# A macaron block of MoE, Mamba and MoE on one core: Mamba's norm statistics in two groups, the first layer's gated sums in four PSUM banks among the first chunk's projections, half of the B diagonals on GpSimd

## Chip, cores, metric

One core of a Trainium2 chip. The metric is the device time of one execution in microseconds, lower is better; the time before is the median of three runs, 862.25 us (859.62 to 864.14).

## What is computed

The input X holds 4096 tokens (16 sequences of 256) of 128 features. Three layers follow, each on the layer norm of X and added to X:

```python
x = x + 0.5 * ffn(layernorm(x))        # mixture of experts
x = x + mamba(layernorm(x))
x = x + 0.5 * ffn(layernorm(x))

# ffn: 64 experts, top 3 of each token, capacity 64, hidden 512
logits = xf @ gate_w + gate_b
top_l, top_i = top_k(logits, 3); gates = softmax(top_l)
h = gelu(buf @ w1 + b1); y = h @ w2 + b2        # buf: tokens by expert
out[token] += gate * y[expert, place]

# mamba: 256 channels, 16 states, kernel 4
raw, gate = split(x @ W_in)
h = silu(causal_conv(raw) + conv_b)
ts, B, C = split(h @ W_x)
dt = softplus(ts @ W_dt + b_dt)
state[t] = exp(dt*A) * state[t-1] + dt*B*h       # per channel and state
y = (sum_n state*C + h*D) * silu(gate);  out = y @ W_out
```

## The kernel before

Five instruction streams are written out by hand, one for each engine and one for the DMA queue of SyncE, and meet at semaphores (`wait_ge`, `then_inc`; helper `wait`). Each engine takes its stream strictly in order, so the place of an operation in the program is its place in the queue.

**MoE layers** (`moe_sync`, `moe_scalar`, `moe_tensor`, `moe_vector`, `moe_pool`, argument f = 0 or 1). X lies in SBUF as 32 tiles of 128 tokens. After the experts' outputs were scattered to DRAM, SyncE loads them back in five pieces (`YK`, L364; pieces of 4, 4, 8, 8, 8 tiles, three rows k each). TensorE forms gated sums of three tiles out of four in PSUM, by matmuls with gate diagonals (L546, eight groups g, one PSUM bank for each), VectorE adds a group's sum to X (L688) and the fourth tile by three scalar products (L683); this is `moe_residual`. Together they are called "residual g" here, and L546's groups "sum g".

**The transition to Mamba.** In `mamba_vector`, `ln_vector` (L238) runs the residual of one group ahead of the norm statistics of the group before (`moe_residual_ahead`, L690): bn_stats (L243), bn_aggr (L246) for all 32 tiles, and then the inverse root with its 13 dependent steps on 32 columns (L258 to L267). After that VectorE fills pads (L1059 to L1061), and only then ScalarE's `mamba_scalar` passes its wait for `rstd` (L1023) and normalises the first chunk (L954). `mamba_tensor` waits for `pads` 4 (L889).

**Mamba** runs over eight chunks of 512 tokens, q = 0 to 7, as a software pipeline with 16 steps n a chunk, from q = -2. In iteration q the scans of chunk q run beside the preparation of chunks b = q+1 and f = q+2:

- f: ScalarE normalises four tiles (L954), TensorE transposes (L783), ScalarE copies (L962), TensorE projects the raw half in two parts (`raw`, L791), ScalarE copies with the bias (L970), VectorE adds the taps of the convolution (L1077, six), ScalarE applies silu (L981), TensorE projects x (`x_proj`, L804), ScalarE copies ts, B and C (L990, L993), TensorE projects dt (L822, two halves) and transposes B (`b_transposes`, L816), ScalarE makes the softplus (L1000 to L1004), VectorE finishes dt (L1083, two halves, steps 14 and 15).
- b: GpSimd multiplies dt by h (`dtu`, L1150), TensorE transposes that (L833), ScalarE copies (L1008), SyncE sends dt and C through DRAM to spread them over partitions (L771, L775, L751, L760).
- q: in each step TensorE forms dt·B·h of a step by 64 small matmuls against the B diagonals (`dbu`, L849) two steps ahead, ScalarE the decays (L1019) four steps ahead, VectorE scans (L1097), GpSimd multiplies the states by C (`times_c`, L1143), TensorE sums over the states (`sum_states`, L871) once four such products are there.

The **B diagonals** are four tensors of 128x1024 a chunk, `dB[b % 2][:, k]`: a constant pattern `fold64` times B's transposed columns, each spread over 64. VectorE makes all four, straight from PSUM bank 4: k = 0 and 1 in steps 14 and 15 of iteration f-2, each ahead of the dt of that step, k = 2 and 3 in steps 0 and 1 of the next:

```python
if n <= 1 and back:
    diagonal(b, 2 + n)
...
if n >= 14 and front:
    diagonal(f, n - 14)
    dt(f, n - 14)
```

A scan waits for the product of GpSimd two scans back (three state buffers), `dbu` for the scan two steps back (two pairs of PSUM banks).

## Time and profile before

| | |
|---|---|
| median of three runs | 862.25 us (859.62 to 864.14) |
| the profiled execution | 867.32 us |
| its span, first to last instruction | 865.6 us |
| busy in the span | TensorE 683.7, VectorE 623.0, GpSimd 462.6, ScalarE 419.1 us |
| mean granted TensorE clock | 0.886 of 2.4 GHz |
| first MoE layer with its sums | 0 to about 209 us |
| Mamba, first normalisation to last product | 218.62 to about 651.6 us |
| second MoE layer | about 652 to 865.6 us |

The rows below give start, duration, engine, line of the kernel, operation and tiles. Durations of neighbours on one engine overlap a little, so costs are taken from start to start where they can. PE is TensorE's matmul, PEld its weight load, DVE VectorE, ACT ScalarE, POOL GpSimd. An idle time in brackets names what released the engine.

### The profile page before, as it was taken

Reading aid. Unit: us, or ns where it says so; the run is one execution under the profiler, and the core shown is the slowest. Engines: PE = TensorE matmul, PEld = TensorE weight load, DVE = VectorE, ACT = ScalarE, POOL = GpSimd, SP = SyncE. Lnnn points to the kernel's source line nnn. Section 1 sums busy time; section 2 is a strip of 40 time slices with the busy share of each in tenths; the row PEclk is TensorE's granted clock in tenths of the full one; section 3 lists DMA queues with packets and bytes.
Section 4 is the critical chain, followed back from the end, with each engine's and each line's share of the span. In section 5 each row is a group of like instructions: output and inputs, shape, how many; then the busy total and the mean of one; then the engine's idle time right before and its main releaser. Section 6 shows DMA issues by size and latency. Waiting matters only on the chain. (4 is left out here: it accounts for less than half of the span.)

```text
span 865.6 us, 27705 instructions
## 1 busy us (share of the span) xinstructions
PE 683.7 (79%) x11818; PEld 426.1 (49%) x11818; DVE 623.0 (72%) x1053; ACT 419.1 (48%) x779; POOL 462.6 (53%) x301
## 2 busy tenths in 40 slices
PE   5637999956456889899798989978886537999967
PEld 3625555545123445446454644545453525555546
DVE  7782555529246989899998989898996891555525
ACT  2410544420457867758676766756531320444520
POOL 3003666420013878798787778878992003566520
PEclk9857999979558999999999999989996757999979
DMA  8992999443055363443425353442004901999537
GB/s 289 396 322 74 341 378 300 160 153 153 5 167 182 120 201 103 140 153 111 154 92 183 111 155 137 114 153 97 3 4 158 396 29 47 329 379 308 181 112 295
DMA packets 92100, 155.47 MB, mean 180 GB/s; under 512 B 7315, under 2 KB 32541, under 8 KB 90704
## 3 DMA queue, kind: packets, MB, share of 16 engines
q1 hardware_dynamic: 87568, 141.40, 48.0%
q0 software_dynamic: 4416, 12.39, 4.1%
q8 instruction: 90, 1.47, 0.7%
q14 instruction: 26, 0.21, 0.1%
HBM read 112.02 MB, written 41.99 MB: 178 GB/s over the span
## 5 line engine op out<-in xcount | busy, mean ns | idle before, releaser
L1143 POOL TENSOR_TENSOR BIG<-BIG,R 128x1024 f32<-128x1024 f32 x128 | 301.1, 2372 | 65.5 <-DVE BIG L1097 65.4
L1097 DVE TENSOR_TENSOR_SCAN BIG<-BIG,ps 128x1024 f32<-128x1024 f32 x128 | 286.0, 2271 | 4.2 <-PE ps L849 2.9
L849 PE MATMUL ps<-BIG,stack 64*32 64x128 f32 x8192 | 154.1, 282 | 48.6 <-DVE BIG L1097 46.8
L849 PEld LDWEIGHTS ps<-BIG,stack 64*32 64x32 f32 x8192 | 118.9, 108 | 125.4 <-DVE BIG L1097 100.7
L1019 ACT ACTIVATE BIG<-BIG,An 128x510 f32<-128x510 f32 x192 | 124.0, 708 | 10.2 <-DVE BIG L1097 9.7
L717 POOL DMA_INDIRECT R<-xn_dram,tok_idx x64 | 65.2, 1019 | 100.7 <-DVE row_idx L645 80.9
L731 POOL DMA_INDIRECT y_dram<-BIG,row_idx x64 | 64.6, 1010 | 69.0 <-DVE BIG L669 63.3
L654 DVE COPY BIG<-ps 128x512 f32<-128x512 f32 x64 | 44.3, 692 | 74.1 <-PE ps L501 74.1
L390 ACT ACTIVATE BIG<-BIG 128x512 f32<-128x512 f32 x64 | 40.4, 631 | 104.9 <-DVE BIG L661 104.9
L871 PE MATMUL ps<-BIG,fold 128*32 128x512 f32 x512 | 70.1, 623 | 5.0 <-POOL BIG L1143 5.0
L501 PE MATMUL ps<-BIG 128*64 128x512 f32 x240 | 68.6, 651 | 0.0
L527 PE MATMUL ps<-BIG 128*64 128x128 f32 x960 | 65.7, 279 | 0.0
L1150 POOL TENSOR_TENSOR state_more<-state_more,BIG 128x512 f32<-128x512 f32 x16 | 20.4, 1274 | 82.3 <-DVE state_more L1083 82.3
L1065 DVE TENSOR_TENSOR BIG<-fold,ps 128x1024 f32<-128x1024 f32 x32 | 38.4, 1204 | 35.1 <-PE ps L816 35.1
L511 PEld LDWEIGHTS ps<-ident,BIG 128*128 128x128 f32 x256 | 36.0, 209 | 52.5 <-issue 52.5
L527 PEld LDWEIGHTS ps<-BIG 128*64 128x64 f32 x960 | 51.2, 136 | 4.0
L384 ACT ACTIVATE BIG<-ps 128x128 f32<-128x128 f32 x64 | 16.8, 262 | 68.8 <-PE ps L491 68.3
L511 PE MATMUL ps<-ident,BIG 128*128 128x128 f32 x256 | 48.5, 313 | 0.0
L661 DVE TENSOR_TENSOR BIG<-ps,b1T 128x512 f32<-128x512 f32 x64 | 44.3, 692 | 4.1 <-PE ps L511 1.4
L1077 DVE SCALAR_TENSOR_TENSOR BIG<-ps,vcol,BIG 128x506 f32<-128x506 f32 (+2 forms) x48 | 34.8, 739 | 14.3 <-ACT BIG L970 13.6
L479 PE MATMUL ps<-BIG 128*64 128x64 bf16 x384 | 24.7, 308 | 24.9 <-DVE BIG L607 24.9
L1019 ACT ACTIVATE BIG<-R,An 128x510 f32<-128x510 f32 x64 | 41.5, 710 | 1.8 <-DVE BIG L1097 1.7
(153 smaller groups left out, 972.4 us busy)
## 6 DMA issues: line engine op xcount, KB each, us to landing
BIG<-in_L_ffn_w SPq DMA_DIRECT2D x120, 512.0 KB, 6.3
dt_dram<-state_more SPq DMA_DIRECT2D x16, 1024.0 KB, 4.3
BIG<-dt_dram SPq DMA_DIRECT2D x48, 256.0 KB
BIG<-y_dram SPq DMA_DIRECT2D x18, 512.0 KB, 9.2
R<-c_dram SPq DMA_DIRECT2D x32, 256.0 KB
y_dram<-zeros SPq DMA_DIRECT2D x3, 2048.0 KB, 17.3
y_dram<-zeros SPq DMA_DIRECT2D x6, 1024.0 KB, 9.7
xn_dram<-R POOLq DMA_DIRECT2D x2, 2048.0 KB, 11.0
```

The source lines that it names most:

```text
L501: last = nc.tensor.matmul(ps[a * CAP:(a + 1) * CAP, 1 + s % 2, :], xt[s % 2][:, a * CAP:(a + 1) * CAP], w1s[b][:, a, :], start=True, stop= ...
L511: last = nc.tensor.transpose(ps[:, 3 + s % 2, c * P:(c + 1) * P], hs[s % 2].rearrange("n (p c) -> n c p", c=HC)[:, c, :], ident[:, :])
L527: last = nc.tensor.matmul(ps[a * CAP:(a + 1) * CAP, 5 + s % 2, 0:D], hT[s % 2][:, c, a * CAP:(a + 1) * CAP], w2s[b][:, a, c, :], start=Fal ...
L654: nc.vector.tensor_copy(hs[s % 2], ps[:, 1 + s % 2, :]).then_inc(S("hs"), 1)
L661: nc.vector.tensor_tensor(hb[s % 2].rearrange("p (c n) -> p c n", n=CAP), ps[:, 3 + s % 2, :].rearrange("p (c n) -> p c n", n=CAP), bias, ...
L717: nc.gpsimd.indirect_dma_start(xg[s], None, xn_dram[f], bass.IndirectOffsetOnAxis(tok_idx[:, j:j + 1].bitcast(U32), 0), bounds_check=T - 1 ...
L731: nc.gpsimd.indirect_dma_start(y_dram[f], bass.IndirectOffsetOnAxis(row_idx[:, j:j + 1].bitcast(U32), 0), yo[s], None, bounds_check=K * T ...
L849: last = nc.tensor.matmul(ps[CW * slot:CW * slot + CW, 2 * (st % 2) + b, :] .rearrange("p (g s k) -> p k g s", g=2, k=4)[:, k], dT[q % 2][ ...
L871: last = nc.tensor.matmul(ps[CW * j:CW * j + CW, 4 + h, :], fold32[:, :], prod[(st + j) % RP][:, :, g, :], start=False, stop=(gp == 1 and ...
L1019: last = nc.scalar.activation(dA[:, st % 6, :, g, 1:SEQ], dtR[cg][:, :, 1:SEQ], ACT.Exp, scale=An4[:, cg, 2 * gp + g:2 * gp + g + 1])
L1097: nc.vector.tensor_tensor_scan(state[st % 3], dA[:, st % 6].rearrange("p b g t -> p (b g t)"), ps[:, u:u + 2, :].rearrange("p b n -> p (b ...
L1143: nc.gpsimd.tensor_tensor(prod[st % RP], state[st % 3].rearrange("p (b g t) -> p b g t", b=2, g=2), Cf[q % 2][:, 2 * gp:2 * gp + 2].rearra ...
```

## The change

- **Statistics in two groups.** The root moves into `inverse_root(e, S, i0, i1, n)`, for any range of tiles. VectorE's Mamba stream takes residuals 0 and 1, the statistics and root of tiles 0 to 7, residuals 2 to 4; in iteration q = -2 it takes residual 5 at step 7, residuals 6 and 7, the last pad and the statistics of tiles 8 to 31 at step 9 (behind the taps), and their root at step 15, ahead of the second dt. Three pads come first. ScalarE waits for the first root ahead of chunk 0 and for the second ahead of chunk 2.
- **Sums in four banks.** In the first layer TensorE's sums leave `moe_tensor`: groups 0 to 3 run ahead of the Mamba iteration, group 4 at step 3 (behind the first transposes), 5, 6 and 7 at steps 6 to 8 (behind the raw projections). Group g uses bank g % 4 in both layers and waits, from group 4, for residual g-4.
- **B diagonals.** ScalarE copies B's transposed columns from PSUM to the new SBUF tile `BT` (128x64) at step 14, between the two softplus parts. VectorE makes k = 0 and 1 from `BT` at steps 0 and 1, GpSimd k = 2 and 3 at steps 3 and 9, each ahead of its product. Steps 14 and 15 of VectorE have none.

The diff, without the lines that only move the root's steps:

```diff
@@ -133,6 +133,7 @@
         fold32 = sb("fold32", [P, CW])
+        BT = sb("BT", [P, 4, NS])
@@ -152,11 +153,11 @@
         row_idx = sb("row_idx", [P, PAIRS], I32)
+        rs = sb("rs", [P, 3, NI])
         rows = small[0:E, 0:H]
-        rs = small[:, 512:608].rearrange("p (m i) -> p m i", m=3)
@@ -226,14 +227,34 @@
         moe_sems, ln_sems = Sems(ctx, nc, "e"), Sems(ctx, nc, "l")
+        MST = M.again(0, STAT_TOTALS)
         LNS = [ln_sems.again(n, LN_TOTALS) for n in range(2)]
-        LST = [ln_sems.again(n, STAT_TOTALS) for n in range(3)]
+        LST = [ln_sems.again(n, STAT_TOTALS) for n in range(2)]
+        def inverse_root(e, S, i0, i1, n):
+            def step(instruction):
+                nonlocal n
+                n += 1
+                instruction.then_inc(S("rstd"), 1)
+                e.wait_ge(*S.at("rstd", n))
+            v, y, z, r = rs[:, 0, i0:i1], rs[:, 1, i0:i1], rs[:, 2, i0:i1], rstd[:, i0:i1]
+            step(nc.vector.tensor_scalar(v, mv[:, i0:i1, 1], EPS, None, ALU.add))
...
+            step(nc.vector.scalar_tensor_tensor(out=nmr[:, i0:i1], in0=mv[:, i0:i1, 0], scalar=-1.0, in1=r,
+                                                op0=ALU.mult, op1=ALU.mult))
@@ -245,27 +266,9 @@
...
             e.wait_ge(*S.at("meanvar", NI))
...
+            inverse_root(e, S, 0, NI, 0)
@@ -364,7 +367,7 @@
         def moe_scalar(e, S, LS, f, between=None):
-            ln_scalar(e, LS, LST[2 * f])
+            ln_scalar(e, LS, LST[f])
@@ -537,19 +540,26 @@
-            e.wait_ge(*S.at("gdiag", MOE_TOTALS["gdiag"]))
-            e.wait_ge(*S.at("yo", PAIRS))
-            for g in range(8):
-                e.wait_ge(G(f"yk{PIECE[g]}"), 16 * K * (f + 1))
-                for i in range(4 * g, 4 * g + 3):
-                    for k in range(K):
-                        last = nc.tensor.matmul(ps[:, g, (i % 4) * P:(i % 4 + 1) * P],
-                                                gdiag[k][:, P * i:P * i + P], YK[:, k, i, :],
-                                                start=(k == 0), stop=(k == K - 1))
-                last.then_inc(S("sum"), 1)
+            if f == 1:
+                for g in range(8):
+                    gate_sums(e, S, f, g)
+        def gate_sums(e, S, f, g):
+            if g == 0:
+                e.wait_ge(*S.at("gdiag", MOE_TOTALS["gdiag"]))
+                e.wait_ge(*S.at("yo", PAIRS))
+            e.wait_ge(G(f"yk{PIECE[g]}"), 16 * K * (f + 1))
+            if g >= 4:
+                e.wait_ge(*S.at("x", g - 3))
+            for i in range(4 * g, 4 * g + 3):
+                for k in range(K):
+                    last = nc.tensor.matmul(ps[:, g % 4, (i % 4) * P:(i % 4 + 1) * P],
+                                            gdiag[k][:, P * i:P * i + P], YK[:, k, i, :],
+                                            start=(k == 0), stop=(k == K - 1))
+            last.then_inc(S("sum"), 1)
         def moe_vector(e, S, LS, f, before_stats=None):
-            ln_vector(e, LST[2 * f], before_stats)
+            ln_vector(e, LST[f], before_stats)
@@ -685,17 +695,7 @@
                     t = X[:, 4 * g:4 * g + 3, :].rearrange("p i d -> p (i d)")
-                    nc.vector.tensor_tensor(t, t, ps[:, g, 0:3 * D], ALU.add).then_inc(S("x"), 1)
-        def moe_residual_ahead(e, S, i):
-            if i % 4 == 0:
-                if i == 0:
-                    moe_residual(e, S, 0, 0)
-                if i + 4 < NI:
-                    moe_residual(e, S, 0, i // 4 + 1)
-                e.wait_ge(*S.at("x", i // 4 + 1))
-                e.wait_ge(*S.at("x4", K * (i // 4 + 1)))
+                    nc.vector.tensor_tensor(t, t, ps[:, g % 4, 0:3 * D], ALU.add).then_inc(S("x"), 1)
@@ -756,6 +756,8 @@
                     wait(e, "prod", STEPS * (b - 1))
+                    if b == 0:
+                        e.wait_ge(*F[0].at("sum", 8))
@@ -811,7 +813,7 @@
                 wait(e, "y", 2 * b - 3)
-                wait(e, "diag", 4 * b)
+                wait(e, "BT", b)
@@ -839,8 +841,11 @@
                 wait(e, "scanned", st - 1)
+                if st == 0:
+                    e.wait_ge(*F[0].at("x", 8))
                 if n == 0:
-                    wait(e, "diag", 4 * q + 4)
+                    wait(e, "diag", 2 * q + 2)
+                    wait(e, "diag_pool", 2 * q + 2)
@@ -855,7 +860,7 @@
                 if h == 0:
-                    wait(e, "diag", min(4 * NQ, 4 * q + 8))
+                    wait(e, "BT", min(NQ, q + 2))
@@ -886,7 +891,9 @@
-            e.wait_ge(M("pads"), 4)
+            for g in range(4):
+                gate_sums(e, F[0], 0, g)
+            e.wait_ge(M("pads"), 3)
@@ -904,6 +911,8 @@
                         transposes(f)
+                    if q == -2 and n in (3, 6, 7, 8):
+                        gate_sums(e, F[0], 0, max(4, n - 1))
@@ -949,6 +958,8 @@
                 wait(e, "t_psum", q)
+                if q in (0, 2):
+                    wait(e, "rstd", STAT_TOTALS["rstd"] * (1 + q // 2))
@@ -1003,6 +1014,13 @@
+            def bt_copy(b):
+                wait(e, "bt_psum", b + 1)
+                wait(e, "diag", 2 * b)
+                wait(e, "diag_pool", 2 * b)
+                nc.scalar.activation(BT[:, :, :], ps[:, 4, 0:4 * NS].rearrange("p (k n) -> p k n", k=4), ACT.Copy)\
+                    .then_inc(M("BT"), 1)
@@ -1015,13 +1033,16 @@
                 wait(e, "scanned", st - 5)
+                if st == 0:
+                    e.wait_ge(*F[0].at("sum", 8))
+                    e.wait_ge(*F[0].at("x4", K * 8))
+                    wait(e, "pads", 4)
-            e.wait_ge(*LST[1].at("rstd", STAT_TOTALS["rstd"]))
-            e.wait_ge(M("pads"), 4)
+            e.wait_ge(M("pads"), 3)
@@ -1048,22 +1069,55 @@
                     if n == 14 and front:
+                        bt_copy(f)
         def mamba_vector(e):
-            ln_vector(e, LST[1], lambda i: moe_residual_ahead(e, F[0], i))
+            def stats(i0, i1):
+                for i in range(i0, i1):
+                    if i % 4 == 0:
+                        e.wait_ge(*F[0].at("x", i // 4 + 1))
+                        e.wait_ge(*F[0].at("x4", K * (i // 4 + 1)))
+                    nc.vector.bn_stats(st[:, i, :], X[:, i, :]).then_inc(M("stats"), 1)
+                for i in range(i0, i1):
+                    wait(e, "stats", i + 1)
+                    nc.vector.bn_aggr(mv[:, i, :], st[:, i, :]).then_inc(M("meanvar"), 1)
+            def statistics(i0, i1, n):
+                wait(e, "meanvar", i1)
+                inverse_root(e, MST, i0, i1, n)
             nc.vector.memset(ts[DTR:DTR + 1, :], 1.0).then_inc(M("pads"), 1)
-            nc.vector.memset(dA[:, :, :, :, 0:1].rearrange("p u b g t -> p (u b g) t"), 0.0).then_inc(M("pads"), 1)
+            for g in range(2):
+                moe_residual(e, F[0], 0, g)
+            stats(0, 8)
+            statistics(0, 8, 0)
+            for g in range(2, 5):
+                moe_residual(e, F[0], 0, g)
+            def rest_of_moe(n):
+                if n == 7:
+                    moe_residual(e, F[0], 0, 5)
+                if n == 9:
+                    for g in range(6, 8):
+                        moe_residual(e, F[0], 0, g)
+                    e.wait_ge(*F[0].at("sum", 8))
+                    e.wait_ge(*F[0].at("x4", K * 8))
+                    nc.vector.memset(dA[:, :, :, :, 0:1].rearrange("p u b g t -> p (u b g) t"), 0.0).then_inc(M("pads"), 1)
+                    stats(8, NI)
+                if n == 15:
+                    statistics(8, NI, STAT_TOTALS["rstd"])
             def diagonal(b, k):
-                wait(e, "bt_psum", b + 1)
+                wait(e, "BT", b + 1)
+                wait(e, "dbu", STEPS * (b - 1))
                 nc.vector.tensor_tensor(dB[b % 2][:, k], fold64[:, :].unsqueeze(1).broadcast_to([P, NS, 64]),
-                                        ps[:, 4, NS * k:NS * k + NS].unsqueeze(2).broadcast_to([P, NS, 64]), ALU.mult)\
+                                        BT[:, k, :].unsqueeze(2).broadcast_to([P, NS, 64]), ALU.mult)\
@@ -1098,15 +1152,18 @@
-            wait(e, "pads", 4)
                 for n in range(STEPS):
+                    if q == -1 and n == 0:
+                        wait(e, "pads", 4)
+                    if q == -2:
+                        rest_of_moe(n)
                     if n <= 1 and back:
-                        diagonal(b, 2 + n)
+                        diagonal(b, n)
@@ -1117,7 +1174,6 @@
                     if n >= 14 and front:
-                        diagonal(f, n - 14)
@@ -1150,10 +1206,21 @@
+            def diagonal(b, k):
+                wait(e, "BT", b + 1)
+                wait(e, "dbu", STEPS * (b - 1))
+                nc.gpsimd.tensor_tensor(dB[b % 2][:, k], fold64[:, :].unsqueeze(1).broadcast_to([P, NS, 64]),
+                                        BT[:, k, :].unsqueeze(2).broadcast_to([P, NS, 64]), ALU.mult)\
+                    .then_inc(M("diag_pool"), 1)
                         dtu(q + 1, n)
+                    if n in (3, 9) and q + 1 >= 0 and q + 1 < NQ:
+                        if q == -1:
+                            e.wait_ge(*F[0].at("sum", 8))
+                        diagonal(q + 1, 2 + n // 9)
```

## Rows read from the trace of the kernel before

**Rows 1.** Stretches (busy us and instruction count of each engine; at the end PEclk, DMA share, GB/s).

```profile
184.00:218.62 34.62, 18.13 (x144) 17.78 (x144) 22.50 (x113) 0.00 (x0) 0.00 (x0) 0.80 0.49 183
...
218.62:244.30 25.68, 12.96 (x20) 4.58 (x20) 7.94 (x11) 14.21 (x23) 1.26 (x1) 0.50 0.12 23
...
244.30:271.00 26.70, 16.86 (x158) 9.18 (x158) 10.29 (x12) 18.12 (x29) 2.54 (x2) 0.68 0.52 168
...
271.00:319.40 48.40, 37.14 (x1107) 20.87 (x1108) 45.49 (x31) 36.05 (x57) 37.93 (x17) 0.96 0.52 175
...
369.00:418.60 49.60, 43.60 (x1157) 25.12 (x1142) 46.69 (x33) 35.55 (x56) 40.11 (x19) 0.98 0.42 135
...
567.40:609.20 41.80, 36.79 (x1072) 21.72 (x1056) 39.24 (x23) 26.32 (x39) 37.87 (x18) 0.95 0.29 104
...
609.20:651.60 42.40, 34.35 (x1048) 20.41 (x1048) 37.17 (x20) 20.15 (x29) 40.30 (x18) 0.95 0.01 3
```

**Rows 2.** Timeline of the transition (start us, us, engine line op out<-in xcount [idle before <-releaser]).

```profile
196.69 0.49 PE L546 MATMUL ps<-BIG,R 128*128 128x128 f32 x2 [1.04 <-DMA BIG<-y_dram]
...
196.81 0.87 DVE L243 BATCH_NORM_STATS2 st<-X 128x6 f32<-128x128 f32 x4
...
208.41 0.61 PE L546 MATMUL ps<-BIG 128*128 128x128 f32 x4
...
209.78 0.87 DVE L243 BATCH_NORM_STATS2 st<-X 128x6 f32<-128x128 f32 x4
...
212.19 0.86 DVE L243 BATCH_NORM_STATS2 st<-X 128x6 f32<-128x128 f32 x4
...
213.25 0.84 DVE L243 BATCH_NORM_STATS2 st<-X 128x6 f32<-128x128 f32 x4
...
214.66 0.18 DVE L258 TENSOR_SCALAR stack<-mv 128x32 f32<-128x32 f32 x1
...
217.61 0.08 DVE L1059 MEMSET R<- 128x6 f32 x2
...
218.62 1.65 ACT L954 ACTIVATE R<-X,nmr,rstd 128x128 f32<-128x128 f32 x4 [37.86 <-DVE BIG L1061]
```

**Rows 3.** The same timeline, the chain of chunk 0.

```profile
220.41 1.09 PE L783 MATMUL ps<-ident,R 128*128 128x128 f32 x4 [11.39 <-ACT R L954]
...
222.66 3.78 PE L791 MATMUL ps<-R,Wr 128*128 128x512 f32 x4 [1.16 <-ACT R L962]
...
225.66 4.53 DVE L1077 SCALAR_TENSOR_TENSOR BIG<-ps,vcol,BIG 128x506 f32<-128x506 f32 x6 [7.16 <-ACT BIG L970]
...
231.33 3.73 PE L804 MATMUL ps<-BIG,Wx 128*96 128x512 f32 x4 [4.89 <-ACT BIG L981]
...
243.61 0.69 DVE L1083 SCALAR_TENSOR_TENSOR state_more<-ps,state_more 128x512 f32<-128x512 f32 x1
```

**Rows 4.** VectorE's timeline, the end of chunk 1's chain and the first scan.

```profile
270.40 0.69 DVE L1083 SCALAR_TENSOR_TENSOR state_more<-ps,state_more 128x512 f32<-128x512 f32 x1 [1.21 <-ACT state_more L1004]
...
271.00 2.28 DVE L1097 TENSOR_TENSOR_SCAN BIG<-BIG,ps 128x1024 f32<-128x1024 f32 x1
```

**Rows 5.** Timeline of a full chunk: TensorE, ScalarE, VectorE.

```profile
384.43 1.07 PE L871 MATMUL ps<-BIG,fold 128*32 128x512 f32 x8
...
387.41 1.53 DVE L1077 SCALAR_TENSOR_TENSOR BIG<-ps,vcol,BIG 128x506 f32<-128x506 f32 x2 [0.21 <-ACT BIG L970]
...
410.71 0.63 ACT L1004 ACTIVATE state_more<-state_more 128x512 f32<-128x512 f32 x1
...
412.25 0.65 PE L816 MATMUL ps<-ident,R 16*128 16x16 f32 x4
...
412.94 1.22 DVE L1065 TENSOR_TENSOR BIG<-fold,ps 128x1024 f32<-128x1024 f32 x1 [2.63 <-PE ps L816]
```

**Rows 6.** Groups of instructions by line (busy us, mean ns of one, idle before, releaser).

```profile
L1143 POOL TENSOR_TENSOR BIG<-BIG,R 128x1024 f32<-128x1024 f32 x128 | 301.1, 2372 | 65.5 <-DVE BIG L1097 65.4
...
L1065 DVE TENSOR_TENSOR BIG<-fold,ps 128x1024 f32<-128x1024 f32 x32 | 38.4, 1204 | 35.1 <-PE ps L816 35.1
```

More of the change, by code:

```diff
@@ L235, in macaron @@
         w2v = w2.rearrange("(a j) (p c) d -> j p a (c d)", a=2, c=HC)
+        def inverse_root(e, S, i0, i1, n):
[6 more added lines that the diff above has]
+            step(nc.vector.tensor_scalar(v, mv[:, i0:i1, 1], EPS, None, ALU.add))
+            step(nc.vector.tensor_single_scalar(z.bitcast(I32), v.bitcast(I32), 1, ALU.arith_shift_right))
+            step(nc.vector.tensor_scalar(r.bitcast(I32), z.bitcast(I32), -1.0, float(0x5F3759DF), ALU.mult, ALU.add))
+            for k in range(3):
+                step(nc.vector.tensor_tensor(y, r, r, ALU.mult))
+                step(nc.vector.scalar_tensor_tensor(out=z, in0=y, scalar=-0.5, in1=v, op0=ALU.mult, op1=ALU.mult))
+                step(nc.vector.scalar_tensor_tensor(out=r, in0=z, scalar=1.5, in1=r, op0=ALU.add, op1=ALU.mult))
+            step(nc.vector.scalar_tensor_tensor(out=nmr[:, i0:i1], in0=mv[:, i0:i1, 0], scalar=-1.0, in1=r,
+                                                op0=ALU.mult, op1=ALU.mult))
         def ln_vector(e, S, before_stats=None):
@@ L246, in ln_vector @@
                     nc.vector.bn_aggr(mv[:, i, :], st[:, i, :]).then_inc(S("meanvar"), 1)
-            n = 0
-            def step(instruction):
-                nonlocal n
-                n += 1
-                instruction.then_inc(S("rstd"), 1)
-                e.wait_ge(*S.at("rstd", n))
-            v, y, z = rs[:, 0, :], rs[:, 1, :], rs[:, 2, :]
-            e.wait_ge(*S.at("meanvar", NI))
-            step(nc.vector.tensor_scalar(v, mv[:, :, 1], EPS, None, ALU.add))
-            step(nc.vector.tensor_single_scalar(z.bitcast(I32), v.bitcast(I32), 1, ALU.arith_shift_right))
-            step(nc.vector.tensor_scalar(rstd[:, :].bitcast(I32), z.bitcast(I32), -1.0, float(0x5F3759DF),
-                                         ALU.mult, ALU.add))
-            for k in range(3):
-                step(nc.vector.tensor_tensor(y, rstd[:, :], rstd[:, :], ALU.mult))
-                step(nc.vector.scalar_tensor_tensor(out=z, in0=y, scalar=-0.5, in1=v, op0=ALU.mult, op1=ALU.mult))
-                step(nc.vector.scalar_tensor_tensor(out=rstd[:, :], in0=z, scalar=1.5, in1=rstd[:, :],
-                                                    op0=ALU.add, op1=ALU.mult))
-            step(nc.vector.scalar_tensor_tensor(out=nmr[:, :], in0=mv[:, :, 0], scalar=-1.0, in1=rstd[:, :],
-                                                op0=ALU.mult, op1=ALU.mult))
+            e.wait_ge(*S.at("meanvar", NI))
+            inverse_root(e, S, 0, NI, 0)
         def ln_normalise(e, S):
```

## Prediction

> **What bounds the kernel now.** I read the stretches first [rows 1]. From the first state scan to the last product the Mamba part takes 380.6 us (271.00 to 651.60). In a full chunk VectorE is busy 46.69 of 49.60 us, TensorE 43.60, GpSimd 40.11, ScalarE 35.55. VectorE sets the pace, with the other two close behind. The last two stretches, where no projections are left, have GpSimd at 37.87 of 41.80 and 40.30 of 42.40: there it is GpSimd. Ahead of the scans lie 26.70 and 25.68 us in which no engine is busy for more than 19 us: a chain from engine to engine, at a granted clock of 0.68 and 0.50 (1.2 GHz in all of the second stretch). Before those, 34.62 us with ScalarE and GpSimd idle, in which VectorE adds the expert outputs and makes the statistics of all 32 tiles.
>
> The timeline of that transition [rows 2] shows the order to be broken: ScalarE's first normalisation starts at 218.62, although the tiles that it needs were complete on VectorE at 196.81. TensorE's last gated sum ends at 209.0. The timeline of a full chunk [rows 5] shows the one stall of VectorE in it: 2.63 us ahead of the first diagonal of step 14, released by the B transposes on TensorE.
>
> **The change, part by part. 1: the early start.** VectorE now takes residuals 0 and 1 (done at 196.81 in both kernels), eight tiles of statistics, then the root. Four tiles of statistics and aggregates take 213.25-212.19 = 1.06, so 2.1 to 198.9. The root takes 217.61-214.66 = 2.95 for 32 columns; eight columns shorten it little, I take 2.8, so 201.7. ScalarE starts at 201.8, 16.8 us earlier than at 218.62. Its four activations take 1.65: 203.5.
>
> TensorE meanwhile: six groups of sums took 209.0-196.69 = 12.3, 2.05 each, at full clock. Groups 2 and 3 end at 200.8, then it waits 2.7 us. Transposes at 203.5 take 0.7 (half of [rows 3] rounded up; 1.09 there at 1.2 GHz), sum 4 2.0 to 206.2, both raw projections half of 3.78 = 1.9 to 208.1, sum 5 to 210.2, sums 6 and 7 to 214.3.
>
> VectorE: a residual costs 212.19-209.78-1.06 = 1.35. Residuals 2 and 3 end at 204.5; residual 4 waits for sum 4 and ends at 207.4. From the end of the first raw half to the first tap there are 1.1 us (222.66+1.9 to 225.66 [rows 3]), the copy on ScalarE: 208.2. Taps, 4.53 for six: two to 209.7; residual 5 waits for sum 5, ends 211.4; four taps to 214.4. Before, x_proj followed the taps by 1.14 (230.19 to 231.33), took 3.73 at 1.2 GHz, and the second dt started 8.55 after its end (243.61), with a diagonal in between. Now: 215.6, 217.5 at full clock (219.3 at 1.2 GHz), and a second dt that is ready by 226.0 (227.9).
>
> Behind those taps VectorE carries the work that it did ahead of them before: residuals 6 and 7 (2.7), a memset (0.1), 24 tiles of statistics (6.4): 223.6. Then dt of the first half (0.7), the second root (2.95), dt of the second half (0.7): it starts at 227.2 and ends at 227.9. So the cover that the early start gave is used up by VectorE itself; ScalarE and TensorE, even with x_proj at 1.2 GHz, are just in time. Before, this dt ended at 243.61+0.69 = 244.30. **Part 1 gives 16.4 us.** If TensorE runs the transposes, sums 4 and 5 and the raw projections at 1.2 GHz, they take 0.4+4.1+1.9 = 6.4 us more, and the gain is 10.
>
> The chain of chunk 1 up to the first scan (26.70 [rows 4]) stays. On it ScalarE gets the BT copy, at most the 0.4 us that one of the four activations at 218.62 takes: 0.25.
>
> **2: four PSUM banks.** Sums 4 to 7 now wait for residuals 0 to 3. In the first layer these are done by 204.5; in the last layer the sums follow their loads (the last group of sums is released by the last load, residual 3 is long done). Nothing. The scratch tile `rs` costs nothing; the new waits on SyncE and ScalarE (for `sum` 8, `x4`, `pads`) are met by 224, over 20 us ahead of their users.
>
> **3: the diagonals, chunks 0 to 5.** Steps 14 and 15 of VectorE lose a diagonal each. At step 14 the dt can start once ScalarE has its softplus, 410.71+0.63 = 411.34, instead of after the stall and the diagonal (412.94+1.14 = 414.08). It ends at 411.95. Step 15's scan ends at 414.15. The second softplus now waits for the B transposes (412.25+0.65) and the copy of BT, and comes to 415.0; its dt ends at 415.6. The next chunk's scan started at 418.60. So 2.95 us less, 46.65 a chunk, if GpSimd keeps up.
>
> GpSimd gets two products of 128x1024 a chunk. Nearest row: 2.37 [rows 6] for the same size in f32 from SBUF. Its inputs here are both broadcast; bounds 1.2 (VectorE's own time for it) and 4.7 (twice). I take 2.37, the row of the same engine and size. Busy then 40.11+4.74 = 44.85 of 46.65: tight. Its first diagonal stands ahead of product 3. Product 2 starts when scan 2 ends, 8.8 us into the chunk (three scans of 2.2 and two diagonals of 1.1; the starts overlap the durations by under 0.1), so product 3 ends at 8.9+3x2.35 = 15.95. TensorE wants it for the sum that started 15.4 into the chunk (384.43-369.00), behind which the raw projection and the tap at 387.41 are queued. The tap moves by 0.55, and the chunk becomes 47.2.
>
> **4: two engines at one memory.** VectorE's diagonals read BT from SBUF now, no longer from PSUM. In a chunk every VectorE instruction of before takes one input at most from SBUF as a tensor, while GpSimd is busy 81% of the time; no row shows a VectorE instruction with two SBUF tensors beside a GpSimd product. Bounds for each of the two meetings a chunk: 0 (no effect), and 2.37, a whole product. I take 1.1, the diagonal's own length, borne by GpSimd: VectorE's diagonal follows its scan at once, and the product that waits for that scan's semaphore comes second. Then product 0 starts at 3.35 instead of 2.3 and the next diagonal pushes by 1.1 again: product 3 ends at 17.4, 2.0 behind the 15.4, and a chunk takes 48.65.
>
> The Trainium skill, page "SBUF — State Buffer", section "Who interferes with whom", speaks against this change: a VectorE instruction with two SBUF inputs and a GpSimd instruction that reads SBUF shut each other out for the whole instruction, whoever comes first. By it the sum would be as above, or 2 to 3 us dearer where GpSimd comes first. No run here shows it yet.
>
> **5: the sum.** First scan: 227.9+26.7+0.25+1.1 (GpSimd's second dtu meets a VectorE diagonal) = 256.0, **15.0 earlier**. Chunk 0 has no Mamba residual (0.6) and took 48.40: now 48.1, 0.3 less. Chunks 1 to 5: 5x(49.60-48.65) = 4.7. In chunk 6 VectorE saves nothing and GpSimd has 37.87+4.74+1.1 = 43.7 for 41.80: 1.9 worse; chunk 7 starts with GpSimd about 1 us further behind: 1.0 worse. Together 15.0+5.0-2.9 = 17.1. The profiled execution took 867.32 (span 865.6), 5.1 above the median 862.25; its 850.2 is 845 on the scale of the median.
>
> **The rivals.** *A, no meeting cost.* A chunk takes 47.2 (chunk 0 46.6): 16.1+1.8+5x2.4-2.1 = 27.8, **835**. For it: VectorE's diagonal, 1.20 on the mean [rows 6] with GpSimd mostly busy, takes 1.22 at 412.94, where GpSimd has nothing to do. Against it: that diagonal reads PSUM.
>
> *B, the clock.* TensorE idles 2.7 us at 200.8 and its clock, full until the end of the sums before (0.80 mean in the first stretch, 0.50 in the next), could fall by then. 6.4 less: **851**.
>
> *C, slower than before.* GpSimd's product of two broadcast inputs costs more than 2.37. Each extra us sits twice in seven chunks, behind product 3 and product 9; of the two about 1.5 come through in a chunk: 10 us in all. At 4.1 us a diagonal the 17 us are gone, at the bound of 4.7 it is 845+23 = **868**. For it: no row has such inputs. Against it: Cf's product has four-dimensional inputs already, and takes 2.37.
>
> *D, the change doesn't do what it says.* The statistics of the other 24 tiles stand ahead of dt in VectorE's order, so the early start only moves the wait. With both roots and a late softplus on top of one another part 1 gives 9 or less, and with meetings of 2.4 us nothing comes from the chunks: within 4 us of before, **859**.
>
> **How the numbers follow.** Forecast (840 to 850) 0.50, A 0.23, B 0.12, D 0.08, C 0.07. A measurement of this kernel can tell about 0.5%, 4.3 us. Faster by more than that (below 857.9): the forecast, A, B and a third of D, 0.88. Same: the rest of D and a mild C (3.7 to 4.5 us a diagonal), 0.07. Slower: 0.05. The range takes in A at its lower side (833) and B with 5 us for a diagonal of 2.9: 857. That leaves out under 2 in 10.
>
> **What would show it.** First normalisation at 202 and first scan at 256 in the span of the profile after; VectorE's dt of the second half at 227 right behind a root. VectorE's stall ahead of the step-14 dt shrinks from 2.63 to about 1. GpSimd's diagonals last 2.4. Meetings show as a VectorE diagonal or a GpSimd product longer than its usual, or a late product 0, and chunks of 48.6 rather than 47.2. TensorE at sum 4 granted below 1.00 means B. The prediction is wrong if chunks take more than 49.6, or if the first scan comes after 262.

## The result and the profile of the changed kernel

The changed kernel takes **842.94 us** (median of 4 runs, 839.05 to 845.3) against 863.19 (859.62 to 871.1) of the kernel before in the same measurement: a ratio of **0.9759, 95% interval 0.972 to 0.9797**, faster by 20 us. The prediction said 845.0, with 833 to 857 as its range. The profiled execution took 839.05 (span 837.3, mean granted clock 0.904); it is the fastest of the four, and the profiled execution before (867.32) lies above its median.

The page's table of engines, kernel after:

```profile
span 837.3 us, 27782 instructions
PE 673.3 (80%) x11818; PEld 421.9 (50%) x11818; DVE 611.5 (73%) x1050; ACT 420.6 (50%) x787; POOL 505.6 (60%) x317
```

The stretches of the kernel after, in the columns of [rows 1]: from the first residual to ScalarE's first normalisation; to the end of the second dt of chunk 0; to the first scan; chunk 0; a full chunk; and the last two chunks.

```profile
186.73:200.02 13.29, 11.39 (x72) 11.04 (x72) 7.31 (x38) 0.00 (x1) 0.00 (x0) 0.77 1.01 392
200.02:228.20 28.18, 16.62 (x92) 12.43 (x92) 23.43 (x94) 14.35 (x24) 1.26 (x1) 0.80 0.19 51
228.20:254.72 26.52, 16.93 (x157) 9.19 (x158) 9.10 (x11) 18.23 (x30) 8.15 (x4) 0.64 0.50 160
254.70:302.00 47.30, 39.88 (x1101) 22.35 (x1100) 43.67 (x28) 35.78 (x58) 43.05 (x19) 0.89 0.50 165
397.92:445.87 47.95, 42.39 (x1141) 24.50 (x1141) 44.66 (x31) 35.78 (x58) 45.48 (x21) 1.00 0.43 140
541.70:583.50 41.80, 34.45 (x1056) 20.68 (x1056) 39.87 (x22) 26.94 (x41) 41.75 (x20) 1.00 0.30 106
583.50:626.50 43.00, 34.43 (x1052) 20.51 (x1052) 37.50 (x20) 20.14 (x29) 41.94 (x19) 0.96 0.02 4
```

In a full chunk GpSimd (45.48) has passed VectorE (44.66), where it stood 6.6 below it. ScalarE's first normalisation started 28.88 after the first residual in the kernel before (218.62-189.74) and starts 13.29 after it now. Where the 28.3 us between the two spans lie, by the starts of the first residual (189.74 and 186.73), the first scan (271.00 and 254.72), chunk 6 and TensorE's last sums over the states:

| stretch | before | after | gain |
|---|---|---|---|
| up to the first Mamba residual | 189.74 | 186.73 | 3.0 |
| first residual to first scan | 81.26 | 67.99 | 13.3 |
| chunks 0 to 5 | 296.36 | 287.02 | 9.3 |
| the last two chunks | 84.30 | 84.74 | −0.4 |
| the rest (second expert layer) | 213.95 | 210.8 | 3.1 |

The first and last rows are expert layers. The change leaves the first alone; in the second it touches only the banks of the gated sums, ahead of which TensorE idles for loads (11.0 us, 13.0 before) and for no residual. So 6 of the 28 us are spread between executions, and the Mamba part gives 22.2. All experiments below are read from the first residual on for this reason. Their chips differ in the expert layers too: the kernel before took 865.06, 883.30 and 882.01 on the three of them. The kernel after was profiled on the last, as a2_after: its span is 25.3 us longer than that of the first measurement, and all of it lies in the expert layers, while its full chunks take 47.93.

### The profile page after: what moved, and what is told of

The parts are those of the page before. It is cut to its first block, busy times and chain, and to the rows that moved or that the text cites. A ratio compares the mean times of both kernels' runs of the same rounds, so it can differ in the third digit from the quotient of the medians.

```text
span 837.3 us, 27782 instructions
## 1 busy us (share of the span) xinstructions
PE 673.3 (80%) x11818; PEld 421.9 (50%) x11818; DVE 611.5 (73%) x1050; ACT 420.6 (50%) x787; POOL 505.6 (60%) x317
## 4 chain that ended last, share of the span: by engine, by line
PE 46%; DVE 25%; issue 11%; POOL 9%; DMA 4%; ACT 3%; SPq 1%; POOLq 0%; DVEq 0%; ACTq 0%
DVE BIG L1151 11%; PE ps L504 8%; PE ps L530 8%; POOL BIG L1199 7%; PE ps L854 6%; PE ps L514 5%; PE ps L482 3%; DVE BIG L1131 3%; PE ps L876 3%; DMA BIG<-y_dram 2%; PE ps L494 2%; PE ps L556 2%; POOL BIG L1212 1%; PE ps L806 1%; DVE stack L567 1%
## 5 line engine op out<-in xcount | busy, mean ns | idle before, releaser
L1199 POOL TENSOR_TENSOR BIG<-BIG,R 128x1024 f32<-128x1024 f32 x128 | 306.2, 2423 | 19.2 <-DVE BIG L1151 18.6
L1206 POOL TENSOR_TENSOR state_more<-state_more,BIG 128x512 f32<-128x512 f32 x16 | 28.2, 1759 | 63.0 <-DVE state_more L1137 63.0
L1041 ACT ACTIVATE BIG<-R,An 128x510 f32<-128x510 f32 x64 | 41.5, 709 | 1.8 <-DVE BIG L1151 1.7
L679 DVE COPY BIG<-ps 128x128 f32<-128x128 f32 x64 | 18.7, 292 | 30.9 <-PE ps L530 30.9
```

The costliest lines, as they stand in the source:

```text
L1041: last = nc.scalar.activation(dA[:, st % 6, :, g, 1:SEQ], dtR[cg][:, :, 1:SEQ], ACT.Exp, scale=An4[:, cg, 2 * gp + g:2 * gp + g + 1])
L1199: nc.gpsimd.tensor_tensor(prod[st % RP], state[st % 3].rearrange("p (b g t) -> p b g t", b=2, g=2), Cf[q % 2][:, 2 * gp:2 * gp + 2].rearra ...
```

## The experiments

Ratios are against the kernel before on the same chip, with 95% intervals; the medians of chips A, B and C can't be compared with each other. Nothing is left out of the computation in any of them. The first column of stretches is from the first residual to the first scan, the second the period of chunks 1 to 5, the third chunks 0 to 5 together, the fourth the last two chunks; each is from the one profiled execution. In e7_all and e8_last the period is that of chunks 2 to 5: their chunk 1 took 47.44 and 47.95, which e7b_all, the kernel of e7_all, doesn't repeat.

| kernel | median us | ratio | to first scan | chunk | 0 to 5 | last two |
|---|---|---|---|---|---|---|
| before (first measurement) | 863.19 | 1 | 81.26 | 49.59 | 296.4 | 84.3 |
| after (first measurement) | 842.94 | 0.9759 [0.972, 0.9797] | 67.99 | 47.95 | 287.0 | 84.7 |
| e2_part1, chip A | 851.26 | 0.9854 [0.9818, 0.9891] | 67.77 | 49.59 | 296.9 | 81.5 |
| e3_part2, chip A | 853.89 | 0.9901 [0.9869, 0.9934] | 79.27 | 47.95 | 287.1 | 85.7 |
| e1_psum, chip A | 832.92 | 0.9628 [0.959, 0.9665] | 66.20 | 46.77 | 280.6 | 84.9 |
| e4_late_root, chip A | 841.78 | 0.9746 [0.9703, 0.9789] | 64.41 | 47.94 | 287.0 | 85.8 |
| e5_slot4, chip B | 852.21 | 0.9631 [0.9593, 0.9669] | 68.82 | 46.64 | 280.2 | 83.6 |
| e6_twice, chip B | 882.90 | 0.9988 [0.9965, 1.0011] | 65.28 | 51.86 | 310.8 | 88.7 |
| e7_all, chip B | 846.07 | 0.9564 [0.9531, 0.9597] | 63.94 | 46.63 | 280.0 | 84.1 |
| e8_last, chip B | 848.49 | 0.9583 [0.9552, 0.9614] | 65.50 | 46.63 | 280.4 | 86.3 |
| a2_after, chip C | 858.93 | 0.9727 [0.9695, 0.9758] | 68.60 | 47.93 | 287.0 | 83.7 |
| e1b_psum, chip C | 851.88 | 0.9657 [0.9625, 0.9688] | 66.23 | 46.77 | 280.5 | 82.5 |
| e9_meet, chip C | 851.95 | 0.9642 [0.9601, 0.9683] | 66.00 | 46.64 | 282.0 | 84.8 |
| e7b_all, chip C | 848.39 | 0.9609 [0.9573, 0.9645] | 65.32 | 46.62 | 279.2 | 84.0 |

But for e6_twice and those two chunks, the period of a full chunk is steady to some 0.02 us between executions and chips. The way to the first scan is not: the kernels after, a2_after, e5_slot4 and e6_twice differ nowhere on it but in GpSimd's diagonals, and take 67.99, 68.60, 68.82 and 65.28. Most of that lies ahead of the last tap of chunk 0, which ended 27.22, 26.82, 27.11 and 24.34 after the first residual. From that tap to the first scan they take 40.8, 41.8, 41.7 and 40.9, so small gains are read from there.

**The two halves of the change.** e2_part1 is the kernel after with all four diagonals back on VectorE, from PSUM, where the kernel before has them (two at steps 0 and 1, two ahead of the dts):

```
-                        bt_copy(f)
-                        diagonal(b, n)
+                        diagonal(b, 2 + n)
+                        diagonal(f, n - 14)
-                        diagonal(q + 1, 2 + n // 9)
+                        pass
```

> The transition of the kernel after alone (statistics in two groups, sums in four banks among the projections); all four B diagonals are VectorE's from PSUM, placed as before. Theory: first scan about 13 us nearer to the first residual than before (before 81.3 us from it), chunks of 49.6 as before, so 13 us faster than before: ratio about 0.985. Rival (the diagonals carry most of the gain): 8 us or less.

e3_part2 is the kernel before with the copy of BT, GpSimd's diagonals at steps 3 and 9 and VectorE's at 0 and 1:

```
+                        bt_copy(f)
+                    if n in (3, 9) and q + 1 >= 0 and q + 1 < NQ:
+                        diagonal(q + 1, 2 + n // 9)
-                        diagonal(b, 2 + n)
+                        diagonal(b, n)
-                        diagonal(f, n - 14)
```

> The kernel before with the B diagonals of the kernel after alone (BT copy on ScalarE, two on VectorE from SBUF, two on GpSimd); transition as before. Theory: chunks of 47.95 instead of 49.6, the last two chunks about 0.5 dearer, first scan within 1 us of before: 9 us faster, ratio about 0.990. Rival (the two parts only work together): less than 5 us.

By the medians the early start alone gives 13.8 us and the diagonals alone 11.2; by the ratios 12.6 and 8.6, both with intervals that leave out 1, and together about the 20.8 of the whole change (0.9759). Each moves its own stretch: e2 the way to the first scan (13.5 less) and no chunk (49.59), e3 the chunks (47.95, as in after).

The diagonals also shorten the way to the first scan, since none stands ahead of dt any more. From the last tap to the first scan e3 takes 38.0, against 40.8 in the kernel before. With the early start this gain remains: 40.8 and 41.8 in the two profiles of the kernel after, against 43.0 in e2. The column hides it (67.99 against e2's 67.77), because e2's last tap ended 2.4 earlier (24.80), and that is TensorE's clock and no edit. TensorE had idled 1.67 us in e2 and 1.26 in e6_twice ahead of chunk 0's transposes, and was granted full clock, 2.4 GHz, for the 10 us from there on. The rows are e2's and e6_twice's, in the columns of [rows 1]:

```profile
204.00:214.50 10.50, 10.38 (x80) 9.24 (x80) 8.11 (x18) 5.49 (x9) 0.00 (x0) 1.00 0.02 6
213.50:223.90 10.40, 10.28 (x80) 9.13 (x80) 8.00 (x18) 5.49 (x9) 0.00 (x0) 1.00 0.02 7
```

In the kernel after it had idled 2.67 and ran at 1.2 GHz for 3.5 us of the same stretch (below).

**What the meetings cost.** A meeting is a VectorE diagonal with both inputs in SBUF that runs beside a GpSimd instruction; a chunk has two. e1_psum keeps GpSimd's diagonals but lets VectorE's two read PSUM again (TensorE gets two waits with it, which keep the bank until the diagonals are done):

```
-                wait(e, "BT", b + 1)
+                wait(e, "bt_psum", b + 1)
-                                        BT[:, k, :].unsqueeze(2) ...
+                                        ps[:, 4, NS * k:NS * k + NS].unsqueeze(2) ...
```

> The kernel after, but VectorE's two diagonals a chunk read B's transposed columns from PSUM bank 4 again, as before the change; GpSimd's two still read the SBUF copy BT. Each VectorE diagonal then has one SBUF input. Theory (the two engines shut each other out when VectorE has two SBUF inputs): GpSimd's product 0 goes back from 3.27 to 2.37 and its second dtu from 2.26 to 1.27, the chunk from 47.95 to 46.9 us, the first scan comes 1 us earlier; in all 6 to 8 us faster than the kernel after. Rival (those two GpSimd instructions are longer for another reason, say the copy BT or the bank that their neighbours use): their durations stay, the chunk stays at 47.9, the time is the kernel after's within 1 us.

GpSimd at the head of a full chunk, kernel after:

```profile
398.96 1.27 POOL L1206 TENSOR_TENSOR state_more<-state_more,BIG 128x512 f32<-128x512 f32 x1
400.27 3.27 POOL L1199 TENSOR_TENSOR BIG<-BIG,R 128x1024 f32<-128x1024 f32 x1
403.50 2.27 POOL L1206 TENSOR_TENSOR state_more<-state_more,BIG 128x512 f32<-128x512 f32 x1
```

VectorE in the same stretch:

```profile
400.11 1.20 DVE L1119 TENSOR_TENSOR BIG<-fold,BT 128x1024 f32<-128x1024 f32 x1
403.43 1.19 DVE L1119 TENSOR_TENSOR BIG<-fold,BT 128x1024 f32<-128x1024 f32 x1
```

The same GpSimd instructions in e1_psum:

```profile
348.61 1.28 POOL L1208 TENSOR_TENSOR state_more<-state_more,BIG 128x512 f32<-128x512 f32 x1
349.91 2.39 POOL L1201 TENSOR_TENSOR BIG<-BIG,R 128x1024 f32<-128x1024 f32 x1
352.27 1.27 POOL L1208 TENSOR_TENSOR state_more<-state_more,BIG 128x512 f32<-128x512 f32 x1
```

GpSimd's product takes 3.27 instead of 2.39 and its second dtu 2.27 instead of 1.27; VectorE's diagonal takes its 1.20 either way. That is 1.9 us a chunk, all of it on GpSimd, recorded as a longer instruction and not as idle time. One changed operand ends it: the product beside it is the same, only VectorE's second input now comes from PSUM. The Trainium skill, page "SBUF — State Buffer", section "Who interferes with whom", has the rule that a VectorE instruction with two SBUF inputs and a GpSimd instruction that reads SBUF contend. This trace agrees with it: 3.27 and 2.27 instead of 2.39 and 1.27. Chunks became 46.77, the time 0.9628. On chip C, beside a2_after, e1b_psum is the same kernel again:

> The kernel after, unchanged, timed on one chip with three of the experiments: the change as made. Expected from its first runs: 20 us below the kernel before of the same chip, chunks of 47.95, first residual to first scan 65 to 69 us.

> The kernel with VectorE's diagonals from PSUM once more, on the same chip as the kernel after: 7 to 10 us below it (chunks of 46.77; six times 1.18 is 7.1, and 1 to 2 us ahead of the first scan).

There it is 7.1 us faster than after (851.88 against 858.93), at the lower end of what was expected. By the profiles 6.5 are in chunks 0 to 5 and 2.4 before the first scan.

**Where the 1.9 us reach the end.** They need not: e5_slot4 leaves both meetings as they are and only puts GpSimd's first diagonal one step later, behind product 3 instead of ahead of it.

```
-                    if n in (3, 9) and q + 1 >= 0 and q + 1 < NQ:
+                    if n in (4, 9) and q + 1 >= 0 and q + 1 < NQ:
```

> The kernel after with GpSimd's first diagonal of a chunk at step 4, behind product 3, instead of step 3, ahead of it. The meetings stay. Theory (what the meetings and the diagonal cost comes through at one place, TensorE's wait for product 3, behind which the raw projection and the taps are queued): product 3 ends 1.9 us earlier, the taps start within 0.4 us of VectorE's scan 6, the chunk goes from 47.95 to about 46.7 us, 7 us in all, although GpSimd's product 0 and dtu keep their 3.27 and 2.26. Rival (GpSimd, busy 45.5 us of 47.95, is the bound by its sum of work): the chunk stays above 47.5.

The sum that waits for product 3 on TensorE and the tap that is queued behind it, kernel after (chunk start 397.92):

```profile
414.67 1.06 PE L876 MATMUL ps<-BIG,fold 128*32 128x512 f32 x8 [1.23 <-POOL BIG L1199]
417.64 1.53 DVE L1131 SCALAR_TENSOR_TENSOR BIG<-ps,vcol,BIG 128x506 f32<-128x506 f32 x2 [0.61 <-ACT BIG L981]
```

The same in e5_slot4 (chunk start 406.93), with the product and the dtu that still take their longer times:

```profile
409.29 3.27 POOL L1199 TENSOR_TENSOR BIG<-BIG,R 128x1024 f32<-128x1024 f32 x1
412.52 2.25 POOL L1206 TENSOR_TENSOR state_more<-state_more,BIG 128x512 f32<-128x512 f32 x1
421.72 1.91 POOL L1212 TENSOR_TENSOR BIG<-fold,BT 128x1024 f32<-128x1024 f32 x1
422.38 1.06 PE L876 MATMUL ps<-BIG,fold 128*32 128x512 f32 x8
425.36 1.53 DVE L1131 SCALAR_TENSOR_TENSOR BIG<-ps,vcol,BIG 128x506 f32<-128x506 f32 x2 [0.21 <-ACT BIG L981]
```

After, the sum starts 16.75 into the chunk, after a wait for GpSimd, and the tap at 19.72. In e5 the sum starts at 15.45 with no wait and the tap at 18.43, as in the kernel before (15.43 and 18.41 [rows 5]). The chunk falls from 47.95 to 46.64. So in a full chunk the diagonal and the meetings are paid together at one place, product 3, and taking away either is nearly enough (46.77 without the meetings, 46.64 with the later diagonal). The rival, that GpSimd's sum of work is the bound, is out: the work is the same in e5.

**The root.** e4_late_root moves the statistics of the other 24 tiles with their root behind both dts and both VectorE diagonals of chunk 0:

```
-                if n == 15:
-                    statistics(8, NI, STAT_TOTALS["rstd"])
+                    if q == -1 and n == 2:
+                        statistics(8, NI, STAT_TOTALS["rstd"])
```

> The kernel after, with the inverse root of tiles 8 to 31 moved from ahead of the second dt of chunk 0 to step 2 of the next iteration, behind VectorE's two diagonals. Theory (part 1 was bounded by VectorE's own work behind the taps): the second dt of chunk 0 starts at once behind the first, about 3.9 us earlier, the first scan too, and the time is 3 to 4 us below the kernel after's. Rival (the chain through the first dt, its store to DRAM and the loads of the rows bounds the first scan): second dt earlier, first scan unmoved, time the same within 1 us.

This missed: 3 to 4 us were expected, and 0.9746 is not to be told from after's 0.9759. The first scan came 3.6 nearer to the first residual, but 2.0 of that is a last tap that ended earlier in this execution (25.24 against 27.22). From the last tap the second dt starts 3.9 earlier, as expected (9.8 against 13.7), and the first scan only 1.6 (39.2 against 40.8): the chain between them grew from 26.4 to 28.7. e7b_all against e1b_psum says about the same, 1.9. The edit had a price of its own. VectorE, kernel e4:

```profile
220.29 1.25 DVE L1135 SCALAR_TENSOR_TENSOR state_more<-ps,state_more 128x512 f32<-128x512 f32 x2
221.47 4.11 DVE L1117 TENSOR_TENSOR BIG<-fold,BT 128x1024 f32<-128x1024 f32 x2
225.51 1.87 DVE L249 TENSOR_SCALAR rs<-mv 128x24 f32<-128x24 f32 x1
227.41 1.82 DVE L250 TENSOR_SCALAR rs<-rs 128x24 int32<-128x24 int32 x1
229.27 0.18 DVE L251 TENSOR_SCALAR rstd<-rs 128x24 int32<-128x24 int32 x1
```

GpSimd beside it:

```profile
221.04 3.46 POOL L1206 TENSOR_TENSOR state_more<-state_more,BIG 128x512 f32<-128x512 f32 x2 [40.72 <-DVE state_more L1135]
224.47 4.74 POOL L1212 TENSOR_TENSOR BIG<-fold,BT 128x1024 f32<-128x1024 f32 x2
```

The two dts now follow each other without the root between them (3.9 us less between them). But the two diagonals take 4.11, against 3.41 in the kernel after and 2.4 without meetings, and two tensor_scalar on 24 columns take 1.87 and 1.82 where the next takes 0.18. The root ends at 231.62 for it, and chunk 1's first tap, whose copy on ScalarE was done at 230.61, starts at 231.66: 1.0 of the 2.3 us. Where the rest lies is open.

**GpSimd's diagonal.** e6_twice makes each of them twice:

```
+                    .then_inc(M("diag_twice"), 1)
+                wait(e, "diag_twice", 2 * b + k - 1)
+                nc.gpsimd.tensor_tensor(dB[b % 2][:, k], ...
```

> The kernel after with each GpSimd diagonal made twice, one behind the other (the same output). It prices a dear diagonal, the prediction's rival C: 3.8 us instead of 1.9. Theory of the prediction: 10 us for each us of a diagonal, so about 19 us slower than the kernel after, chunks of about 50.5. With the diagonal of step 9 hidden: half of that, chunks of 49.8 or less.

Two full chunks of e6_twice, in the columns of [rows 1]:

```profile
318.50:369.90 51.40, 43.95 (x1140) 25.20 (x1140) 44.66 (x30) 35.79 (x58) 49.25 (x23) 0.97 0.40 130
421.44:473.25 51.81, 43.98 (x1140) 25.05 (x1140) 44.66 (x30) 35.78 (x58) 49.25 (x23) 0.97 0.40 130
```

GpSimd is the bound: 49.25 of 51.40. The chunks take 51.86 on the mean, 3.9 more than after's 47.95 for 3.8 us more of diagonals, and the last two take 88.7, also 4 more. So all of the added work comes through, where 50.5 a chunk was expected. The whole time is that of the kernel before (0.9988): at 3.8 us a diagonal (twice 1.9) the change is worth nothing.

**Together, and two more misses.** e7_all has the edits of e1, e4 and e5; e9_meet those of e4 and e5 and keeps the meetings; e8_last is e7_all with all four diagonals of the last chunk on VectorE, to relieve GpSimd in chunk 6:

```
+                        if b == NQ - 1:
+                            diagonal(b, 2 + n)
-                    if n in (4, 9) and q + 1 >= 0 and q + 1 < NQ:
+                    if n in (4, 9) and q + 1 >= 0 and q + 1 < NQ - 1:
```

> VectorE's diagonals from PSUM, the late second root, and GpSimd's first diagonal at step 4, together on the kernel after. If the three gains are of different places: first scan 5 us nearer to the first residual than in the kernel after (62.7 us), chunks of 46.6; 14 to 16 us faster than the kernel after, 827 us. If the place of GpSimd's diagonal and the meetings are the same loss (TensorE's wait for product 3), the slot adds nothing to the kernel with PSUM reads: chunks of 46.7 against its 46.77, and all of the rest is the late root's 3.5 us.

> The kernel e7 with all four diagonals of the last chunk on VectorE, at steps 0 and 1 of chunk 6, where GpSimd is the bound and VectorE has 2.6 us to spare. Theory: GpSimd loses 3.8 us of work in chunk 6, VectorE's scans 1 and 2 come 1.1 and 2.2 us later; 1 to 3 us off the last two chunks (84.7 to 84.9 us in the kernel after and with PSUM reads). Rival (TensorE's order sets the last two chunks): no change.

> The kernel after with the late second root and GpSimd's first diagonal at step 4, the meetings kept (VectorE's diagonals read SBUF). Theory (in a full chunk the meetings come through only at TensorE's wait for product 3): chunks of 46.64, and within 2 us of the kernel e7, which has no meetings; 10 to 12 us below the kernel after. Rival (the meetings cost time of their own): 3 us or more above e7.

> The kernel e7 (PSUM reads, late root, diagonal at step 4) on the same chip as the kernel after: chunks of 46.63, 11 to 15 us below the kernel after, the fastest of the four.

e7_all has the lowest ratio of the case: 0.9564, and 0.9609 as e7b_all beside a2_after, 10.5 us faster than after (848.39 against 858.93; 11 to 15 were expected). e9_meet gains 7.0 of these, not the 10 to 12 that were expected, and lies 3.6 above e7b_all, where its rival had 3 or more; but its six runs spread from 846.27 to 858.21, and the two ratios overlap. In full chunks the theory holds: its chunks 1 to 5 are as short as e7b_all's (46.64 and 46.62), so reading PSUM brings nothing more there once product 3 is free of the diagonal. The difference of the profiles lies mainly in chunk 0 (48.80 against 46.10), and e9's profile is of its slowest run. e5_slot4, with the meetings too, takes 47.01 there, so the meetings alone don't make the 48.80, and what they cost in chunk 0 stays open. e8_last missed: 0.9583, no better than e7_all. GpSimd, its chunk 6:

```profile
546.99 2.37 POOL L1203 TENSOR_TENSOR BIG<-BIG,R 128x1024 f32<-128x1024 f32 x1 [0.82 <-DVE BIG L1151]
551.43 2.36 POOL L1203 TENSOR_TENSOR BIG<-BIG,R 128x1024 f32<-128x1024 f32 x1 [2.07 <-DVE BIG L1151]
554.20 7.02 POOL L1203 TENSOR_TENSOR BIG<-BIG,R 128x1024 f32<-128x1024 f32 x3 [0.41 <-DVE BIG L1151]
```

With two diagonals in a row on VectorE (546.82, 2.33 for both) the next scan is late, and GpSimd idles 2.07 for it. In all of chunk 6 it is busy 38.2 and idle 7.0, against 40.1 and 1.1 in e7_all: the work that was taken off GpSimd was given back as waits. Part of them may be the clock: from 550 to 560 TensorE was granted 0.78 in e8 and 1.00 in e7_all.

## Why the prediction was right, step by step

**The early start: right in kind, 1.7 us dear in this execution.** Measured from the first residual, the first scan was forecast at 66.3 and came at 67.99, where the kernel before has 81.26. VectorE's second dt came 3.3 later than forecast (41.5 against 38.2 after the first residual), in three pieces. ScalarE's first normalisation came 1.2 later (13.29 against 12.06): TensorE's first gated sums ran at a granted clock of 0.50 (1.2 GHz) until about 192, so residual 1 was late. Then a small form of rival B, a further 1.3 up to the last tap. Stretches of the kernel after:

```profile
186.73:192.00 5.27, 5.16 (x24) 5.19 (x25) 1.26 (x4) 0.00 (x0) 0.00 (x0) 0.50 1.02 367
195.20:199.00 3.80, 3.80 (x36) 3.75 (x34) 3.49 (x25) 0.00 (x0) 0.00 (x0) 1.00 1.03 418
199.00:201.80 2.80, 0.14 (x2) 0.02 (x1) 2.59 (x11) 1.65 (x4) 0.00 (x0) 1.00 0.42 167
201.80:204.00 2.20, 2.19 (x16) 2.20 (x17) 1.21 (x4) 1.10 (x2) 0.00 (x0) 0.78 0.00 2
204.00:208.00 4.00, 4.00 (x16) 2.76 (x16) 1.37 (x4) 0.93 (x2) 0.00 (x0) 0.69 0.00 0
208.00:214.00 6.00, 5.84 (x53) 5.65 (x51) 5.59 (x11) 3.47 (x7) 0.00 (x0) 1.00 0.01 3
```

TensorE idles 2.7 us for ScalarE's normalisation, is granted 0.78 and 0.69 behind it, and then full clock again. Rival B had it at 1.2 GHz for all of sums 4 and 5 and the raw projections, at a price of 6.4 us. It ran at 1.2 GHz for 3.5 us (0.51 from 203.0 to 206.5), and that cost 1.3 against the forecast. Against e2 and e6_twice, which were at full clock there, it is 1.6: from the first normalisation to the end of the last tap they take 12.3, the kernel after 13.9. The third piece is the root, in VectorE's own work behind the taps (0.8 net):

```profile
197.52 0.17 DVE L250 TENSOR_SCALAR rs<-rs 128x8 int32<-128x8 int32 x1
...
223.14 0.66 DVE L1137 SCALAR_TENSOR_TENSOR state_more<-ps,state_more 128x512 f32<-128x512 f32 x1
...
223.92 1.26 DVE L250 TENSOR_SCALAR rs<-rs 128x24 int32<-128x24 int32 x1
225.21 0.18 DVE L251 TENSOR_SCALAR rstd<-rs 128x24 int32<-128x24 int32 x1
...
227.59 0.69 DVE L1137 SCALAR_TENSOR_TENSOR state_more<-ps,state_more 128x512 f32<-128x512 f32 x1
```

L250 takes 1.26 while GpSimd's dtu runs from 223.88 to 225.14. The order itself is as forecast: dt, root, dt, VectorE just in time. Back came 1.5: the chain from there to the first scan took 26.52, not 28.05. The meeting in it (GpSimd's second dtu 2.17, not 1.27) is there: without it e1 has 25.63, and on chip C a2_after 27.51 and e1b_psum 25.66. What the step missed is the other side, that VectorE's diagonals no longer stand ahead of chunk 1's dts either; e2, where they do and no meeting is, takes 0.8 more than e1. All of this is within what the way to the first scan varies: the forecast of 66.3 lies between the 65.28 of e6_twice and the 68.82 of e5_slot4.

**Four banks: nothing, as said.** e2, which has them, takes 49.59 a chunk, as before, and in the last layer none of TensorE's idle time ahead of the sums is put down to a residual.

**The diagonals, and the price of one.** The floor of 46.65 a chunk "if GpSimd keeps up" was met to 0.02 us by e5, e7 and e9. GpSimd's diagonal was taken at 2.37 and takes 1.97 on the mean, 1.90 undisturbed. This term was mis-sized. Groups by line, kernel after:

```profile
L1212 POOL TENSOR_TENSOR BIG<-fold,BT 128x1024 f32<-128x1024 f32 x16 | 31.5, 1968 | 0.0
L1119 DVE TENSOR_TENSOR BIG<-fold,BT 128x1024 f32<-128x1024 f32 x16 | 20.2, 1269 | 0.0
```

**The meetings.** Forecast at 1.1 each, borne by GpSimd; measured at 0.9 and 1.0 in product 0 and the second dtu, borne by GpSimd. Only ahead of chunk 0 did GpSimd come first, and then VectorE bore it: its two diagonals at 228.20 took 3.41. With both sizes put right (0.47 less for the diagonal and 0.3 less for the meetings) the forecast chunk of 48.65 becomes 47.9; 47.95 was measured. Where they come through was right: the sum behind product 3, forecast at 17.4 into the chunk, came at 16.75. Chunks 0 to 5 gave 9.3 instead of 5.0.

**The last two chunks** were to be 2.9 worse; the two profiles say 0.4. Kernels with the same program there differ by nearly 3: 84.3 and 81.5 for the two with VectorE's four diagonals (before, e2), 83.6 to 85.8, mean 84.7, for the six with GpSimd's two and the meetings (e5 and e9 with the first of them a step later). By these it is some 1.8 worse, and that GpSimd's diagonals do come through there is shown by e6: 88.7, with 3.8 us more of them. The term stands; its size stays open within that spread. Its working also has a slip: chunk 6 has two meetings, and the sum counts one.

**The sum.** 15.0+5.0−2.9 = 17.1 was forecast; 22.2 lie in the changed part of the profiled executions and 20 in the runs. The early start gave 1.7 less than its 15.0, the chunks 4.3 more, the end 2.5 more in this pair of profiles; the errors partly offset each other. That 845.0 came within 2.1 us of the median is partly that luck: the stretches were off by up to 4.3. *Rival A* (no meeting cost) was wrong as a mechanism: the meetings exist. Its chunk of 47.2 is nearly that of e1, in which they are gone (46.77). *Rival C* is refuted in its premise (1.9, not over 3.7). Its break-even of 4.1 us a diagonal is about what e6 shows (3.8), but by two errors that offset: each us more of a diagonal was to cost 10 us in all and costs about 12 (e6's ratio is 0.023 to 0.026 above that of the kernel after, 20 to 23 us, for 1.9 us), and the gain that it eats up was larger. *Rival D* falls with e2 and e3, both of which gain alone.

## What to carry to other kernels

When work moves from the busiest engine to one nearly as busy, its price is not its duration but what it delays: here two GpSimd diagonals and two meetings cost 1.3 us a chunk only because one diagonal stood ahead of the product that TensorE's queue waits for, and one slot later they were free. Leave in PSUM one of the two inputs of a VectorE tensor_tensor that runs beside GpSimd: it was worth 7.1 us with the diagonal in the bad slot, and nothing in a full chunk with it in the good one. When a chain is started earlier, look for what VectorE did ahead of it for nothing: it now stands between the chain's links. And where executions of one program differ by 3.5 us in a stretch, as here up to the first scan, read a small gain from a nearer event.
